# One release wait per expert for Gelu, and new order lists for the main and the last pass

## The reference

```
x = x + attention(norm(x))   # 16 heads of 8: out = (rot_q rot_k' / (q k')) v, no softmax
x = x + ffn(norm(x))         # shared expert + top 2 of 8 experts, 128 -> 512 -> 128, exact gelu
x = x + scan(norm(x))        # Mamba block: conv, dt = softplus, h = exp(dt A) h + dt B x, 16 states
x = x + ffn(norm(x))         # the same ffn weights
```

## Time and profile before

| | us |
|---|---|
| median of 3 runs (lowest to highest) | 4017.41 (4011.95 to 4021.06) |
| the profiled execution, its own time | 4019.45 |
| its span, first to last instruction | 4017.3 |
| PE busy in the span | 3458.3 (86%) |
| ACT busy | 3227.9 (80%) |
| DVE busy | 2936.5 (73%) |
| POOL busy | 1559.3 (39%) |
| mean granted TensorE clock | 0.931 of full speed |

### The profile page before, as it was taken

One profiled execution on the slowest core, in us unless ns is written; L12 is line 12 of the kernel. 1 busy time (PEld: TensorE's weight loads), 2 busy tenths in 40 slices (PEclk: granted clock), 3 DMA queues, 4 the chain that ended last, 5 costly groups with the idle time before them and its releaser, 6 DMA issues.

```text
span 4017.3 us, 38974 instructions
## 1 busy us (share of the span) xinstructions
PE 3458.3 (86%) x11446; PEld 1464.2 (36%) x11446; DVE 2936.5 (73%) x3513; ACT 3227.9 (80%) x4037; POOL 1559.3 (39%) x758
## 2 busy tenths in 40 slices
PE   3786698989899898989989898989989898898847
PEld 1141233434333343433334343433334343344424
DVE  2427768788696868879696877869697886959592
ACT  3677688888888888988989888888988888886653
POOL 1112235435253544425253543524354442415261
PEclk9586799999999999999999999999999999998978
DMA  4142445544444545444544444545454444434432
GB/s 147 45 136 61 128 144 150 156 141 141 149 145 147 152 136 162 144 143 140 155 146 145 147 145 151 147 140 149 145 155 139 150 140 150 145 108 139 131 129 71
DMA packets 214852, 552.05 MB, mean 137 GB/s; under 512 B 25105, under 2 KB 96626, under 8 KB 214642
## 3 DMA queue, kind: packets, MB, share of 16 engines
q1 hardware_dynamic: 214642, 549.57, 44.8%
HBM read 488.65 MB, written 63.18 MB: 137 GB/s over the span
## 4 chain that ended last, share of the span: by engine, by line
PE 47%; DVE 19%; ACT 16%; issue 13%; POOL 4%; DMA 1%; SPq 1%; ACTq 0%; POOLq 0%; DVEq 0%
PE bank L782 15%; PE bank L734 5%; PE bank L771 5%; ACT rPool L884 4%; ACT L1022 4%; DVE ws L1220 4%; PE bank L712 4%; PE bank L673 4%; DVE rPool L1108 4%; PE bank L773 3%; PE bank L772 3%; PE bank L707 3%; DVE ws L1227 3%; ACT hF L884 3%; DVE ws L1216 2%
## 5 line engine op out<-in xcount | busy, mean ns | idle before, releaser
L782 PE MATMUL bank<-hF,wst 128*128 128x512 f32 x2304 | 1212.1, 643 | 68.3 <-DVE tmp L1178 62.6
L1108 DVE TENSOR_TENSOR rPool<-bank,rPool 128x512 f32<-128x512 f32 x1024 | 700.2, 684 | 461.1 <-PE bank L712 431.8
L884 ACT ACTIVATE hF<-bank,cols 128x512 f32<-128x512 f32 x1152 | 771.2, 687 | 249.7 <-PE bank L773 240.5
L1328 POOL TENSOR_TENSOR yM<-yM,ws 128x1024 f32<-128x1024 f32 x240 | 742.6, 3094 | 471.9 <-DVE ws L1227 461.1
L1313 POOL TENSOR_TENSOR acc<-acc,tmp 128x512 f32<-128x512 f32 x240 | 442.6, 1844 | 1123.1 <-DVE tmp L1178 1116.8
L884 ACT ACTIVATE rPool<-bank 128x512 f32<-128x512 f32 x1040 | 574.9, 594 | 271.2 <-PE bank L707 217.9
L1220 DVE TENSOR_TENSOR_SCAN ws<-dAs,ws 128x1024 f32<-128x1024 f32 x256 | 696.7, 2722 | 4.1 <-ACT dAs L884 1.5
L1022 ACT ACT_TABLE_LOAD x531 | 681.3, 1283 | 9.4
L771 PE MATMUL bank<-xnH,wst 128*128 128x512 f32 x1152 | 625.9, 543 | 73.0 <-ACT hF L884 69.8
L782 PEld LDWEIGHTS bank<-hF,wst 128*128 128x128 f32 x2304 | 426.1, 200 | 505.8 <-issue 368.9
L712 PE MATMUL bank<-qpk,kpk 48*128 48x512 bf16 x1024 | 421.4, 412 | 178.8 <-DVE rPool L1108 177.3
(11 more groups left out here) (154 smaller groups left out, 3031.9 us busy)
## 6 DMA issues: line engine op xcount, KB each, us to landing
wst<-wscr SPq DMA_DIRECT2D x288, 768.0 KB, 5.6
bc<-bcscr SPq DMA_DIRECT2D x256, 512.0 KB, 4.1
cB<-gscr SPq DMA_DIRECT2D x256, 256.0 KB, 4.7
qscr<-parts SPq DMA_DIRECT2D x192, 128.0 KB, 5.1
kscr<-parts SPq DMA_DIRECT2D x192, 128.0 KB, 2.1
kpk<-kscr SPq DMA_DIRECT2D x128, 192.0 KB, 5.9
qpk<-qscr SPq DMA_DIRECT2D x128, 192.0 KB, 6.4
wscr<-wst SPq DMA_DIRECT2D x9, 512.0 KB, 2.6
```

The lines of the kernel that those rows point to most:

```text
L782: pe.matmul(ps[FFN][:, :], w2, hF[:, q % HSLOTS, :], start=(c == 0), stop=(c == FC - 1)).then_inc(s_dn, 1)
L884: return nc.scalar.activation(out_, in_, fn, **kw)
L1108: v.tensor_tensor(rP[:, step % 2, c, :], ps[NUM][:, :], rP[:, step % 2, c, :], ALU.mult).then_inc(s_mul, 1)
L1328: g.tensor_tensor(yM[:, :, :], yM[:, :, :], ws[:, s % 3, :, :], ALU.add).then_inc(s_ya, 1)
```

## The change

Two things change. A gelu waits for the release of its tiles only at the first chunk of an expert, there for all four tiles at once (the down 9 chunks back instead of 12), and the other three chunks of an expert wait for their up alone. And the texts of `MAIN` and `LAST` are replaced on all five engines. They hold the same steps the same number of times, but for table loads: `MAIN` has 17 `T.gelu` where it had 16, and `LAST` has 24 `T.gelu` and 23 `T.log` where it had 19 and 19. The other texts stay.

```diff
-                    act.wait_ge(s_dn, floor(NCH * f + n - HSLOTS + 1))
+                    if c == 0:
+                        act.wait_ge(s_dn, floor(NCH * f + n + FC - HSLOTS))
...
 MAIN = {
...
-    A.den H.up*2 A.v H.down*3 A.num A.den*3 H.down H.up F.mean H.down*2 H.up A.den A.num H.down H.up*2 H.down F.var
+    A.v H.down*2 A.den*2 H.up H.down A.den*2 H.down H.up A.num H.down F.mean H.down A.num A.den*2 H.up*6 F.var A.num
```

More of the change, by code:

```diff
@@ L127 @@
     "SP": """
-    N.bc P.in N.bc H.w H.gate N.bc F.w H.gate N.bc F.w*2 H.out N.bc F.rows N.bc F.gate*2 F.w N.bc*2 F.w F.gate N.bc
-    F.gate F.w*2 A.load F.gate*2 F.w P.pk F.w F.gate*2 G.w A.load P.pk G.w G.rows P.pk G.w G.gate*2 M.rows G.w
-    M.bc*2 P.pk M.bc G.w G.gate M.bc P.ahead M.bc G.gate G.w*2 M.bc*2 G.gate*2 G.w P.ahead
+    N.bc P.in N.bc H.w N.bc H.gate*2 F.w*2 N.bc H.out F.w N.bc*2 F.rows F.w F.gate*2 N.bc F.w N.bc*2 A.load F.w
+    F.gate F.w F.gate F.w F.gate*3 F.w P.pk G.w F.gate A.load G.w*2 P.pk*2 G.rows G.w G.gate M.rows M.bc*2 G.w
@@ L150 @@
[L150 to L153, removed]
-    F.gelu P.cast F.gelu*3 T.log A.ln*2 A.ex G.mean A.ln*2 G.var T.gelu F.gelu*2 P.cast F.gelu*2 T.log A.ln*2
@@ L159 @@
+    G.gelu*3 P.cast M.mean T.log M.var A.ex M.xp A.ln*2 M.xp T.gelu G.gelu M.xp G.gelu*2 T.silu M.silu M.xp M.silu*3
+    T.gelu G.gelu*2 M.row T.log A.ln*2 M.dt A.ex A.ln M.dt A.ln M.sp T.gelu G.gelu*2 T.log M.decay A.ln*3 A.ex A.ln
+    M.decay A.ln*2 M.decay A.ex T.gelu G.gelu*2 P.cast G.gelu*4 T.log A.ln*2 M.decay A.ln*2 M.decay A.ex T.gelu
+    G.gelu*2 P.cast G.gelu*2 T.log A.ln*4 A.ex A.ln*2 M.decay A.ln*2 A.ex M.decay T.gelu G.gelu*4 A.oT T.log
 """,
     "DVE": """
-    A.v H.part N.dbx F.mean A.mul N.scan A.mul N.hc H.part N.dbx A.mul N.scan A.mul N.hc H.part F.var N.dbx F.router
@@ new lines @@
+    F.part N.scan P.til A.mul*4 N.dbx A.mul F.part N.hc A.mul N.scan A.mul N.hc F.part E.mean A.mul P.til*2 F.part
+    A.mul*2 E.var A.mul F.part E.gate A.mul G.mean A.mul*3 F.part G.var G.router G.route F.part A.mul G.turn M.mean
+    M.var M.conv*4 A.mul M.conv*4 G.part A.mul*7 M.dt M.dbx*2 M.scan M.hc A.mul G.part A.mul*2 M.scan A.mul M.hc
+    M.dbx A.mul M.scan A.mul*2 M.hc G.part M.dbx A.mul M.scan M.dbx A.mul M.hc A.mul*2 G.part A.mul M.scan A.mul
+    M.hc A.mul*4 G.part A.mul*3 M.dbx*2 M.scan*2 M.hc*2 A.close
@@ L199 @@
+    M.row G.gelu M.dt G.gelu*2 M.dt T.log M.sp M.decay*2 T.gelu G.gelu*2 T.log M.decay T.gelu G.gelu*3 T.log
+    M.decay*2 T.gelu G.gelu T.silu M.silu T.log M.decay*2 T.gelu G.gelu*3 T.log M.decay T.gelu G.gelu*5 T.log
+    M.decay*2 T.gelu G.gelu*5 T.log M.decay T.gelu G.gelu T.log M.decay T.gelu G.gelu*2 T.log M.decay T.gelu
+    G.gelu*3 T.log M.decay T.silu M.silu T.gelu G.gelu*2 T.log M.decay T.gelu G.gelu T.log M.decay G.close
 """,
     "DVE": """
-    F.mean H.part N.dbx N.scan N.dbx N.scan H.part N.hc*2 F.var F.router H.part N.dbx F.route N.dbx H.part N.scan
@@ L207 @@
-    M.scan G.part M.hc M.dbx M.scan M.hc M.dbx M.scan M.hc
+    F.mean N.dbx H.part N.scan N.hc N.dbx H.part N.scan N.dbx N.hc H.part F.var F.router N.dbx H.part N.scan F.route
+    N.hc N.scan F.turn N.hc N.dbx F.part N.scan N.dbx N.hc N.scan F.part N.hc N.dbx N.scan N.hc F.part N.dbx N.scan
+    F.part N.dbx N.hc N.scan F.part N.hc E.mean F.part E.var F.part E.gate G.mean G.var F.part G.router G.route
+    F.part G.turn M.mean M.var M.conv*8 G.part*2 M.dt M.dbx M.scan M.hc M.dbx M.scan M.hc M.dbx M.scan M.hc M.dbx
```

96 lines of the change are left out of this document (44 added, 52 removed).

## The result

The changed kernel takes 3908.1 us (median of 4 runs, 3899.8 to 3910.1), the kernel before 4017.8 (4 runs, 4012.0 to 4021.1). The ratio is 0.9725, with a 95% interval of 0.9707 to 0.9743: 2.7% faster.

The account below looks back on a forecast made before the run. No engine was full; PE was nearest, with 21.6 us idle a pass, plus its lower clock. -1.2 and -1.3 made -2.5 a pass, -32.5 over 13 passes, -34.5 with the last pass: 3985 us, range 3938 to 4044.

Parts of the forecast that it names:

- numerators: Fewer numerators directly behind one another on PE: at most 2.5 us a pass gained, half taken, -1.2.
- downs behind a part and the clock: PE's 2.18 us wait for an expert's part and 1.8 us of slower downs after it: 4.0 a pass, -1.3 taken.
- the gelu side: ACT saves at most 2.2 us a pass on gelu pairs and loses 1.3 to a table load; 0 taken.
- the last pass: Nine more table loads on ACT, fewer PE waits for parts up to the scan: -2 us, bounds -7.1 and +5.
- rival 2: All gains show in full: -6.5 us a main pass, 7 in the last pass, 3928 us; chance 0.08.
- The removed and the added wait: Dropped gelu waits save 0.12 us a pair on ACT, hidden behind PE; the stricter remaining wait costs 0.
- The added load: One more table load on ACT in the main list: +1.3 us a pass as upper bound, 0 taken.
- one slow stretch: Ten microseconds of PE at a lower clock, in one of two neighbouring passes: priced at 2.2 us of the pass.
- the pause at 2049.6: PE stops 2.18 us for an expert's part; it should shrink to nothing and the slow downs after it may go.
- Rival 3: Slower by the clock: more PE pauses, each followed by slow running, 4049 to 4061 us; chance 0.22.
- its moved steps: Steps moved on POOL, which is busy 98 of 231 us a pass, were to cost nothing.
- Rival 1: Stalls come back elsewhere in the chain over three engines: 4017 us, within 8; chance 0.20.

Follow-up runs that it names:

- experiment 1: Kernel before with only the new gelu wait (once per expert), old order lists: 4022.6 us, ratio 1.0006.
- Experiment 15: Changed kernel with two more table loads a main pass, of the table already loaded, inside groups of gelus: 3927.6 us, ratio 0.9762 to the kernel before.
- experiment 16: Changed kernel without the two table loads at the seam of two main passes, 27 fewer in all: 3900.4 us, ratio 0.9694 to the kernel before.
- experiment 7: Changed kernel with four more pairs of numerators directly behind one another on PE in the main list: 3941.8 us, ratio 0.9803 to the kernel before.
- experiment 8: Kernel before with no two numerators directly behind one another on PE in the main list, which also separates ups: 4035.3 us, ratio 1.0041.
- experiment 6: Kernel before with the part that PE waited 2.18 us for moved ahead of its `hc` on DVE: 4023.0 us, ratio 0.9997.
- experiment 9: Changed kernel with three downs near the start of a pass moved back to just behind the previous expert's last down: 3919.4 us, ratio 0.9736 to the kernel before.
- experiment 5: Kernel before with the next expert's part, not the one PE paused for, moved ahead of its `hc` on DVE: 4004.3 us, ratio 0.9960.
- experiments 13 and 14: POOL adds only 64 of 512 tokens of each scan product: in the kernel before 3869.7 us (0.9625), in the changed kernel 3782.2 us (0.9405).
- experiments 3 and 4: New wait with new `MAIN` and old `LAST`: 3926.4 us (0.9762); with old `MAIN` and new `LAST`: 4005.9 us (0.9967); ratios to the kernel before.

## Why the prediction was wrong

**In short.** The sum took a discount from every stall, and this step failed. It counted 1.2 us a main pass for numerators (half of 2.5), 1.3 for downs behind a part and the clock (a third of 4.0), 0 for the gelu side and for POOL, and 2 for the last pass: 34.5 in all. A main pass fell by 7.5 us in the mean, and in the passes shown numerators wait 3.1 us less, downs for parts 2.6 less, ups for gelus 1.5 less, with 2.7 less busy time of PE. The last stretch fell by 22.5. The 6.5 us of rival 2, the same terms with no discount, is nearest for a main pass, though not made of the same parts.

**The removed and the added wait: priced right at 0, for a wrong reason.** The 0.12 us between the gelus of a pair does not belong to the second wait (experiment 1); I had it hidden behind PE, so the error did not reach the sum.

**The added load.** I took 0 with a bound of 1.3 us a pass. Experiment 15 puts two loads a pass in the middle of groups at 1.1 us together, experiment 16 shows no price for those at the seam. The added one of `MAIN` is neither: both texts end with the logarithm's table loaded and open with `T.gelu`, and the new one loads gelu once more right behind the silu steps, where the old one went on to `T.log`. Its price alone was not measured. Nothing contradicts the bound.

**Numerators: the step that failed first.** "Some of the 11 waits must be of that kind [...]. I take half, -1.2." The waits fell from 9.0 to 5.9, by 3.1, which is more than the 1.2 and more than my upper end of 2.5. In the new lists four bare pairs cost 2.2 us a pass by the times (1.4 to 3.0 by the intervals) and 3.1 in most passes of the profile (experiment 7), so 1.2 was too small. In the old lists, taking them apart the way that experiment 8 does made passes 1.5 us longer. The price of a stall was asked of the kernel before, but whether it is paid depends on the order around it.

**Downs behind a part: right in what went, wrong in why it counts.** The wait of 2.2 us has gone, as forecast. Taken away alone in the old lists it is worth 0 (experiment 6). Putting the downs back in the new lists did not bring it back (experiment 9), so what its absence is worth there is not measured. The third that I took (1.3) has no run that shows it.

**The clock.** The price of 2.2 us for one slow stretch holds: experiment 5 took away the one of every second pass; the passes that had it fell by 2.8 us and the others by 0.6. I had tied a slow stretch to the pause at 2049.6, and it doesn't hang on it: without the pause it came ten microseconds later (experiment 6). In the new lists a pass has 2.7 us less of PE busy time with the same products, of the 8.4; I had counted at most 1.8 of it and taken a third. Rival 3, which wanted more such stretches, was wrong in its sign.

**Missing: additions on POOL beside steps on DVE.** I wrote that POOL "has 98 of 231 us busy and its moved steps cost nothing". The changed order makes POOL 18.5 us and DVE 9 us a pass less busy with the same instructions. The earlier trace rows had the 2.72 us `hc` in them; I used it as the reason of a wait and did not ask why a step whose median is 1.23 us took 2.72. The scan additions stand for about 22 of the 110 us (experiments 13 and 14), by the profiles some 13 in the last stretch and about 1 in each main pass. So this omission explains a large part of the miss in the last pass, and little of the miss in the main passes.

**The last pass.** Forecast -2 with a bound of -7.1, measured -22.5: 17 by the new `LAST` and 6 by what the new `MAIN` leaves for it (experiments 3 and 4). The bound was the sum of three waits of PE up to the scan, and it was no bound, since most of the waits that shrank come later. These are PE's longest waits from 3648.7 to 4017.3, before:

```profile
PE bank L782 <- DVE tmp L1178: 28.9, 6, 8.6
PE bank L771 <- ACT hF L884: 23.0, 8, 8.8
PE bank L673 <- POOL yM L1328: 14.7, 1, 14.7
PE bank L787 <- POOL acc L1313: 9.2, 3, 4.8
```

and from 3551.8 to 3897.8, after:

```profile
PE bank L771 <- ACT hF L884: 17.0, 10, 7.8
PE bank L771 <- DMA wst<-wscr: 16.5, 5, 11.3
PE bank L787 <- POOL acc L1314: 14.3, 3, 10.5
PE bank L782 <- DVE tmp L1179: 13.7, 5, 7.7
PE bank L844 <- DVE yM L1245: 6.3, 1, 6.3
PE bank L673 <- POOL yM L1329: 5.8, 1, 5.8
```

I had stopped counting at 3775, at the scan, and wrote that after it "DVE sets the time with the same work". Most of the change is behind it: PE waits for POOL's last scan sum 5.8 us instead of 14.7, and the waits for parts fell by 15, where only 7.1 of the 28.9 lie ahead of 3775. Two waits grew: ups wait 16.5 us for weight tiles, and `close` waits 14.3 for POOL instead of 9.2.

**The sum.** The form was a sum of separate stalls, each discounted because it might come back. No repair of the old lists' order, one at a time or three together, brought more than 1.7 us a pass, and the new lists bring 7.5 in the mean and 8.4 in the shortest passes. Rival 1 describes experiments 6 and 8 well, and rival 2 is nearest to the whole order. Its bound of 6.5 a pass was passed by about 1, its 7 in the last pass by 15.

**What stays open.** Of the 8.4 us between the passes shown, 2.7 are PE's busy time, at a granted clock of 0.99 instead of 0.97 and 0.98, and 5.8 its idle time, of which numerators are 3.1, parts 2.6, gelus 1.5, and the longer wait for POOL takes back 1.3. This says where the time went, not what took it away. The scan additions account for about 1 us of it (experiments 13 and 14); the experts' additions and the other work of POOL beside DVE were not cut in any run. The new `MAIN` text of PE, ACT, DVE or POOL can't stand alone beside the old ones of the other engines: a step of it then waits for one that another's old order holds behind it, and the program stops for good. That of SP could, and was not run. So which engine's text carries the gain is not known.

## What to carry to other kernels

Here all engines' orders were replaced together, and pricing each visible stall of the old order at a discount underestimated the whole. Single repairs shifted a stall or gained little (ratios of 0.996 to 1.004), while the new order, which covers several at once, gained more than the full price of those that I had seen (7.5 against 6.5 us a pass). So for such a change the sum with no discount belongs inside the range, and not at a chance of 0.08; this is one case, and no rule for the size. And a step whose duration in the trace is twice its median is a question to be asked first: here it pointed to additions on POOL, of which seven eighths cost the two kernels 126 and 150 us, more than the whole change gained.

## What the runs showed of the hardware

- A POOL addition and a DVE step with two SBUF inputs shut each other out. In the whole kernel before, 1.2 us becomes up to 3.2 (`hc`), 2.3 up to 4.5 (`scan`), and 2.3 up to 4.4 on POOL (`yM`). Of 327 steps of the scan that began inside an instruction of POOL, all but one took what was left of it plus their own time, less 0.12 to 0.14 us.
- A second semaphore to wait for costs this kernel nothing that shows: 864 waits less, ratio 1.0006.
- The second gelu of a pair starts 0.59 us behind the first, or 0.70 when the first was held for its up (medians of 252 and 225 pairs in the kernel before). Without the second wait (experiment 1) it is the same.
- Ten steady passes in a row of the kernel before repeat, every second one, to a tenth of a microsecond, and so do their slow-clock stretches; those of the changed kernel don't (221.7 to 226.5). One exchange of two DVE steps takes the stretch 180 us into every second pass away in ten of twelve passes (0.97 and 0.98 become 0.98 and 0.98). Removing the longest pause of PE moved the stretch behind it by ten microseconds and left the clock of the pass as it was.
